# Two deformable layers: nine stored taps, the first batch on two queues, the fourth band convolved behind the first nine units

## The chip, the cores and the metric

One core of one Trainium2 chip runs the whole program in one launch. The metric is the device time of one execution in microseconds (us). All data are float32. The engines are TensorE (PE), VectorE (DVE), ScalarE (ACT), GpSimd (POOL) and SyncE (SP); each has its own list of instructions and they wait for each other by semaphores. DMAs are issued from the lists of SP, POOL and, in the changed kernel, ACT.

## The reference

The input is 8 images of 16 channels, 64 x 64. Four layers follow one another: a group norm with a gated scan, a mixture-of-experts inverted residual block, two deformable convolutions with group norm and a residual, and two "distance" convolutions. The change is in the two deformable layers alone, which are alike:

```python
off = conv2d(x, ow, ob).reshape(Bn, K, 2, Hh, Ww)      # K = 9 taps, an offset in y and one in x for each
cy = iy + dy + off[:, :, 0]; cx = ix + dx + off[:, :, 1]
samp = gather(y0i, x0i, (1-wy)*(1-wx)) + ...           # bilinear: four neighbours
out = einsum('bckhw,ock->bohw', samp, w) + b           # then norm over the image, relu, + x
```

## The kernel before, in words

A deformable layer (L is 0 or 1, called the first and the second pass here) does the gather as matrix products. The offsets come from a 3 x 3 convolution that is made in four bands m of 16 image rows. The rest is made in NB = 16 batches n of 4 rows, each in three units (parts of the image's width), 48 units a pass.

**The offsets' way.** PE convolves band m (`convolve`, L1487: 9 taps, 144 products, 288 records). ACT copies it from PSUM (`copy_offsets`, L1202, 4 instructions). DVE clips it (`bound_offsets`, L793 and L795) and, for the check for far taps, reduces the raw values (`reach`, L800). SP stores the clipped band in the DRAM tensor "offsets" (`store_offsets`, L503: 4 DMAs of 256 KB, with 16 planes an image and axis, of which 9 are taps). SP then copies from DRAM to DRAM what a batch needs into "offsets_by_batch" (`arrange_batch`, L520: 10 DMAs for batch 0, of which 4 serve image edges, and 6 for the others). POOL loads a batch to SBUF, each image's data repeated over the rows that need it (`load_batch`, L1737: 4 DMAs of 576 or 624 KB, both axes together, 2.3 to 2.5 MB a batch). There are three buffers for batches, so load n waits until DVE is done with batch n-3.

**The batches.** ACT turns a batch's x offsets into distances (`distances`, L1219) and writes |y| for a unit (`y_terms`, L1226). DVE finishes the distances (L812) and makes for each unit four products (L820 twice, L822, L823). PE multiplies them with windows of the image (`sample`, L1521, L1526); ACT copies the samples out of PSUM (`copy_samples`, L1239, L1242). After two batches PE contracts them with the layer's weights (`contract`, L1545, L1550); ACT and DVE write and add the resulting rows (`copy_rows` L1254, `add_shared_rows` L840). The products of a unit lie in a ring of three (RING), so y_terms of unit i+3 waits for PE's sample of unit i. The windows come from a copy of the image by columns: PE turns it (`turn_columns`, L1499), ACT and DVE copy it (`copy_columns`, L1192 and L1193, L784 and L785), POOL stores it (L1709) and loads windows (`load_windows`, L1724), ACT and DVE spread them (`spread_windows`, L1212 and L459).

**The order is written out by hand**, one list an engine, in the functions below. At a pass's start it is: PE convolve(0), turn_columns 0 to 7, convolve(1), (2), (3), then the units. ACT copy_offsets(0), copy_columns, copy_offsets(1), (2), distances(0), y_terms of units 0 to 2, spread_windows(0), copy_offsets(3), distances(1), spread_windows(1), then the units; before unit 6 it waits until all four bands are stored, because the samples of batches 2 and 3 take the place of the clipped offsets. DVE bound_offsets(0), copy_columns, reach(0), bound and reach of 1 and 2, spread_windows(0), batch 0, bound and reach of 3, then the batches. SP store(0), arrange 0, 1, 2, store(1), store(2), arrange 3, store(3), arrange 4 and so on. POOL store_columns, load_windows(0), load_batch(0), load_windows(1), load_batch(1), then a load for each batch and windows for every second.

## Time and profile before

| | |
|---|---|
| three runs | 735.8, 734.52, 729.37 us; median 734.52 us |
| the profiled execution | 729.7 us, of which the span of the profile is 727.5 us |
| mean granted clock of PE, as a share of full speed | 0.929 |
| busy share of the span: DVE, PE, ACT, POOL | 82%, 79%, 62%, 20% |
| first pass: last input row written, batch 0 begun on DVE (L812) | 174.0, 223.25 us |
| second pass: the same | 408.2, 461.63 us |

Times in rows are in us from the span's start, and durations are in us unless marked ns. A row of the timeline gives start, duration, engine, line, operation, tiles, the count of merged instructions, and in brackets how long the engine had been idle before it and what it waited for. In the chain of waits each row is a piece of the path that ended last. "SPq" and "POOLq" are DMA-issuing instructions.

### The profile page before, as it was taken

Reading aid. Unit: us, or ns where it says so; the run is one execution under the profiler, and the core shown is the slowest. Engines: PE = TensorE matmul, PEld = TensorE weight load, DVE = VectorE, ACT = ScalarE, POOL = GpSimd, SP = SyncE. Lnnn points to the kernel's source line nnn. Section 1 sums busy time; section 2 is a strip of 40 time slices with the busy share of each in tenths; the row PEclk is TensorE's granted clock in tenths of the full one; section 3 lists DMA queues with packets and bytes.
Section 4 is the critical chain, followed back from the end, with each engine's and each line's share of the span. In section 5 each row is a group of like instructions: output and inputs, shape, how many; then the busy total and the mean of one; then the engine's idle time right before and its main releaser. Section 6 shows DMA issues by size and latency. Waiting matters only on the chain.

```text
span 727.5 us, 29228 instructions
## 1 busy us (share of the span) xinstructions
PE 576.0 (79%) x13258; PEld 413.8 (57%) x13258; DVE 600.2 (82%) x853; ACT 453.1 (62%) x803; POOL 146.1 (20%) x258
## 2 busy tenths in 40 slices
PE   2719999999888698888886788669888888659491
PEld 1205887775654477666665454357666666537380
DVE  6998999942459999999998443999999999884866
ACT  2776774233227789999983412669999899251514
POOL 1005000010241343344200025134334420000000
PEclk9959999999988899999999798979999999969696
DMA  5004000000669898888730066979888862000003
GB/s 215 0 9 109 4 5 20 4 5 20 168 219 386 246 310 276 277 276 274 247 130 2 3 178 216 379 235 306 279 287 283 279 222 112 3 1 5 1 4 116
DMA packets 30198, 111.16 MB, mean 153 GB/s; under 512 B 11140, under 2 KB 15940, under 8 KB 25976
## 3 DMA queue, kind: packets, MB, share of 16 engines
q0 software_dynamic: 14912, 87.85, 35.8%
q1 hardware_dynamic: 15160, 21.42, 9.7%
q8 instruction: 105, 1.72, 1.0%
q14 instruction: 21, 0.17, 0.1%
HBM read 92.25 MB, written 19.65 MB: 154 GB/s over the span
## 4 chain that ended last, share of the span: by engine, by line
DVE 38%; PE 36%; DMA 10%; ACT 6%; issue 5%; SPq 2%; POOL 1%; DVEq 0%; ACTq 0%; POOLq 0%
PE psum L1433 12%; DVE arena L820 8%; DVE arena L822 7%; DVE arena L823 7%; DMA arena<-offsets_by_batch 7%; PE psum L1487 6%; PE psum L1642 6%; DVE arena L812 3%; PE psum L1521 3%; ACT arena L1212 2%; PE psum L1451 2%; PE psum L1652 2%; DMA offsets_by_batch<-offsets 1%; PE psum L1391 1%; SPq L520 1%
## 5 line engine op out<-in xcount | busy, mean ns | idle before, releaser
L1521 PE MATMUL psum<-arena 64*64 64x297 f32 (+4 forms) x4512 | 223.1, 340 | 48.3 <-DVE arena L823 40.9
L1521 PEld LDWEIGHTS psum<-arena 64*64 64x64 f32 x4512 | 171.1, 136 | 106.8 <-DVE arena L823 49.6
L1737 POOL DMA_DIRECT2D arena<-offsets_by_batch x128 | 78.1, 624 | 200.0 <-DVE arena L823 130.1
L1239 ACT ACTIVATE arena<-psum 128x396 f32<-128x396 f32 (+1 forms) x192 | 86.1, 509 | 36.4 <-PE psum L1521 24.0
L1487 PE MATMUL psum<-arena 32*32 32x512 f32 x2304 | 88.3, 651 | 22.7 <-issue 16.9
L820 DVE SCALAR_TENSOR_TENSOR arena<-arena 128x396 f32<-128x396 f32 (+1 forms) x192 | 98.2, 554 | 3.5 <-ACT arena L1226 2.5
L1433 PE MATMUL psum<-arena 32*32 32x512 f32 x2592 | 93.6, 597 | 0.0
L822 DVE SCALAR_TENSOR_TENSOR arena<-arena 128x792 f32<-128x792 f32 (+3 forms) x96 | 92.3, 961 | 0.0
L823 DVE SCALAR_TENSOR_TENSOR arena<-arena 128x792 f32<-128x792 f32 (+3 forms) x96 | 92.2, 960 | 0.0
L1545 PE MATMUL psum<-arena 64*64 64x256 f32 x1152 | 83.1, 381 | 2.6 <-ACT arena L1242 2.2
L1487 PEld LDWEIGHTS psum<-arena 32*32 32x32 f32 x2304 | 49.3, 107 | 59.3 <-issue 44.9
L1226 ACT ACTIVATE arena<-arena 128x792 f32<-128x792 f32 (+1 forms) x96 | 81.9, 857 | 0.0
L1219 ACT ACTIVATE arena<-arena 128x2304 f32<-128x2304 f32 (+1 forms) x32 | 71.6, 2236 | 12.3 <-DMA arena<-offsets_by_batch 12.3
L1433 PEld LDWEIGHTS psum<-arena 32*32 32x32 f32 x2592 | 65.1, 102 | 18.3 <-issue 3.5
L1212 ACT ACTIVATE arena<-arena 128x384 f32<-128x384 f32 (+2 forms) x124 | 65.1, 601 | 0.0
L1202 ACT ACTIVATE arena<-psum,arena 128x512 f32<-128x512 f32 x32 | 19.8, 687 | 67.9 <-PE psum L1487 67.8
L793 DVE TENSOR_SCALAR arena<-arena 128x2048 f32<-128x2048 f32 x8 | 10.8, 1347 | 56.6 <-ACT arena L1202 56.6
L716 DVE SCALAR_TENSOR_TENSOR arena<-arena 128x2048 f32<-128x2048 f32 x24 | 56.4, 2349 | 0.5
L1642 PE MATMUL psum<-arena 32*32 32x512 f32 x1152 | 44.4, 663 | 8.6 <-DVE arena L1022 8.6
L1545 PEld LDWEIGHTS psum<-arena 64*64 64x64 f32 x1152 | 43.9, 132 | 11.2 <-ACT arena L1242 2.4
L1151 ACT ACTIVATE arena<-psum,arena 128x512 f32<-128x512 f32 x48 | 34.2, 780 | 22.5 <-PE psum L1391 16.3
L812 DVE TENSOR_SCALAR arena<-arena 128x2304 f32<-128x2304 f32 (+1 forms) x32 | 43.7, 1366 | 1.7 <-ACT arena L1219 1.7
(169 smaller groups left out, 640.8 us busy)
## 6 DMA issues: line engine op xcount, KB each, us to landing
arena<-offsets_by_batch POOLq DMA_DIRECT2D x112, 576.0 KB, 7.9
arena<-offsets_by_batch POOLq DMA_DIRECT2D x16, 624.0 KB, 7.6
offsets<-arena SPq DMA_DIRECT2D x32, 256.0 KB, 10.0
offsets_by_batch<-offsets SPq DMA_DIRECT2D x184, 24.0 KB
arena<-columns POOLq DMA_DIRECT2D x24, 160.0 KB, 9.3
columns<-arena POOLq DMA_DIRECT2D x8, 320.0 KB, 6.7
arena<-in_x SPq DMA_DIRECT2D x4, 512.0 KB, 5.3
out<-arena SPq DMA_DIRECT2D x8, 256.0 KB, 2.2
```

The costliest lines, as they stand in the source:

```text
L820: v.scalar_tensor_tensor(own, own, 1.0, ap(tx + odd * W + u * TW, [[2 * W, KR // 2], [1, 2 * WB[u]]]), ALU.subtract, ALU.mult, reverse0=(o ...
L822: v.scalar_tensor_tensor(term(0), part(ty), 0.0, part(tx), ALU.max, ALU.mult)
L823: v.scalar_tensor_tensor(term(2), part(ty), 0.0, part(tx), ALU.min, ALU.mult).then_inc(s_g, 1)
L1212: ins = nc.scalar.activation(*spread_views(c, a, b, i), ACT.Copy, scale=con("image4", i, 1))
L1226: a.activation(ap(g_at(unit, 1), [[TW, KR], [1, 2 * WB[u]]]), ap(in_at(n, 1) + u * TW, [[W, KR], [1, 2 * WB[u]]]), ACT.Abs).then_inc(s_nd, 1)
L1239: ins = a.activation(ap(to + half * 2 * K * SX, [[SR, 2], [SX, 2 * K], [1, w]]), ap_ps(bank, [[CH, 2], [w, 2 * K], [1, w]], half * 2 * K * ...
L1433: ins = t_.matmul(ps_q(j, dw_bank(step) + i), cols(W_DIAG + (t * K + k) * Q, Q, Q * i, Q), ap(T_PAD[t % 4] + row * PW + k % 3, [[PW, CR], ...
L1487: ins = t_.matmul(ps_q(2 * axis + h, conv_bank(m) + i), cols(W_CONV[L] + (axis * K + t) * Q, Q, Q * i, Q), ap(XA + (BLK * m + 8 * h + t // ...
L1521: ins = t_.matmul(ps_t(s, bank + r, first * K * w, many * K * w), window, ap(g_at(unit, d0) + first * TW + s * w, [[GS + TW, many], [SLOTS ...
L1545: ins = t_.matmul(ps_t(r, bank, (2 - k // 3) * SX, GR * SX), weights_, ap(SAMP + j % 2 * SPAR + r * SR + k * SX, [[K * SX, GR], [1, SX]], ...
L1642: t_.matmul(ps_q(j, 4 * c + i), cols(W_DT[L] + k * P + Q * i, Q, Q * i, Q), at, start=(step == 0), stop=False)
L1737: g.dma_start(cols(in_at(n, 0), 2 * in_rows(n) * W, 64 * r + 32 * half, 32), bass.AP(batch_d.tensor, 2 * (4 * r * NB + n) * INS, [[0, QW / ...
```

## The change

It has five parts, the same in both passes.

1. The DRAM tensor "offsets" has 9 planes an image and axis in place of 16, and a row of zeros above and below each (written once, near the kernel's start, by 4 DMAs on SP). A band is stored by 8 DMAs of 9 partitions x 4 x 2 KB in place of 4 of 32 partitions. The DMAs for the edges at arranging go.
2. The first batch: SP stores, arranges and loads the x axis of band 0 and batch 0, ACT the y axis, each with its own DMAs (4 for the store, 4 to arrange, 4 to load). ACT does the store between copy_columns of groups 0 and 2, and arranging and loading before copy_offsets(1).
3. Every other batch is loaded by POOL with 8 DMAs, x first and then y, with a semaphore an axis; distances waits for x, y_terms of a batch's first unit for y. load_batch(1) now stands ahead of load_windows(1).
4. Band 2: ACT copies it after spread_windows(0), and DVE bounds and reduces it after batch 0 in place of before. Band 3: PE convolves one tap behind each of units 0 to 8, ACT copies it before unit 9, DVE reduces and bounds it after batch 4. The first contraction moves from units 6 to 10 to units 10 and 11, copy_rows(0) to unit 12.
5. SP's order becomes store(0), arrange 0, load x of batch 0, arrange 1, 2, store(1), arrange 3, 4, store(2), arrange 5 to 8, store(3), arrange 9 and on. ACT waits before unit 6 for bands 0 to 2 alone, and before unit 27 for band 3.

```diff
@@ -223,7 +223,7 @@
         xt_d = nc.dram_tensor("columns", [2, XQ, 4, H, C], F32, kind="Internal").ap()
-        off_d = nc.dram_tensor("offsets", [2, B * KP, H, W], F32, kind="Internal").ap()
+        off_d = nc.dram_tensor("offsets", [2, B * K, H + 2, W], F32, kind="Internal").ap()
         batch_d = nc.dram_tensor("offsets_by_batch", [B, NB, 2 * INS], F32, kind="Internal").ap()
@@ -315,7 +317,7 @@
         def conv_bank(m):
-            return 4 if m % 2 == 0 else 0
+            return 0 if m == 1 else 4
         HALF = N // 2
@@ -420,12 +422,14 @@
         def in_count(L, n):
-            return 64 * ((NB + 2 - n % 3) // 3 * L + n // 3 + 1)
+            if n == 0:
+                return 64 * (L + 1)
+            return 64 * ((NB - 1) // 3 * L + (n + 2) // 3)
         def arranged(L, n):
-            return 32 * ((14 if n % 4 in (0, 3) else 12) * L + 3 * (n // 4 + 1) + (2 if n % 4 == 0 or n == NB - 1 else 0))
+            return 32 * ((9, 12, 12, 13)[n % 4] * L + 3 * (n // 4 + (n % 4 > 0)) + (n == NB - 1))
         def g_at(unit, d):
@@ -471,7 +475,39 @@
                      ap_ps(bank, [[SX, rows], [1, WB[2]]], rho * SX + 2 * WB[0])))
+        def bounded_at(m):
+
+            return RAW + NATS if m == 3 else D1 + m % 2 * NATS
+
+        def store_part(eng, L, m, axis):
+
+            for h in range(2):
+                for b in range(2):
+                    eng.dma_start(bass.AP(off_d.tensor, (axis * B + b) * K * PLANE + W + (2 * m + h) * CH,
+                                          [[PLANE, K], [2 * K * PLANE, 4], [1, CH]]),
+                                  ap(bounded_at(m), [[CH, 4], [1, CH]], 64 * axis + Q * h + KP * b, K)
+                                  ).then_inc(s_ds[m], 16)
+
+        def arrange_first(eng, axis):
+
+            for ky, at, step, row, rows in ((-1, 0, SLOTS, 1, SLOTS), (0, 3 * SLOTS, SLOTS, 0, SLOTS),
+                                            (1, 6 * SLOTS, SLOTS, -1, SLOTS), (-1, KR, 1, 0, 1)):
+                eng.dma_start(bass.AP(batch_d.tensor, (axis * ER + at) * W, [[2 * NB * INS, B], [step * W, 3], [1, rows * W]]),
+                              bass.AP(off_d.tensor, (axis * B * K + 3 * (ky + 1)) * PLANE + (row + 1) * W,
+                                      [[K * PLANE, B], [PLANE, 3], [1, rows * W]])).then_inc(s_af[axis], 16)
+
+        def load_part(eng, n, axis):
+
+            for half in range(2):
+                for r in range(2):
+                    eng.dma_start(cols(in_at(n, axis), in_rows(n) * W, 64 * r + 32 * half, 32),
+                                  bass.AP(batch_d.tensor, 2 * (4 * r * NB + n) * INS + axis * in_rows(n) * W,
+                                          [[0, QW // 2], [2 * NB * INS, 4], [1, in_rows(n) * W]])
+                                  ).then_inc(s_in[n % 3][axis] if n else s_fl[axis], 16)
+
         UNITS = NB * NU
+        PLANE = (H + 2) * W
+        OWN_TAPS = NU * 3
         @block.sync
@@ -488,6 +524,10 @@
                                  cols(T_PAD[3], H * C, 0, 4 * HALO)).then_inc(s_zp, 16)
+            for axis in range(2):
+                for row in (0, H + 1):
+                    sp.dma_start(bass.AP(off_d.tensor, axis * B * K * PLANE + row * W, [[PLANE, B * K], [1, W]]),
+                                 cols(T_PAD[0], W, 0, B * K)).then_inc(s_oz, 16)
             for pair in (0, 2):
@@ -498,17 +538,13 @@
                 sp.wait_ge(s_d1, 4 * L + m + 1)
-                for axis in range(2):
-                    for h in range(2):
-                        sp.dma_start(bass.AP(off_d.tensor, axis * B * KP * N + (2 * m + h) * CH,
-                                             [[N, 2 * KP], [2 * KP * N, 4], [1, CH]]),
-                                     ap(D1 + m % 2 * NATS, [[CH, 4], [1, CH]], 64 * axis + Q * h, Q)
-                                     ).then_inc(s_ds[m], 16)
+                for axis in ((0, 1) if m else (0,)):
+                    store_part(sp, L, m, axis)
             def arrange_batch(L, n):
-                sp.wait_ge(s_ds[min(SLOTS * n + SLOTS, H - 1) // BLK], 64 * (L + 1))
+                sp.wait_ge(s_ds[min(SLOTS * n + SLOTS, H - 1) // BLK], 128 * (L + 1))
                 if n >= 4:
@@ -519,20 +555,11 @@
                                              [[2 * NB * INS, B], [step, 3], [1, rows * W]]),
-                                     bass.AP(off_d.tensor, (axis * B * KP + 3 * (ky + 1)) * N + row * W,
-                                             [[KP * N, B], [N, 3], [1, rows * W]])).then_inc(s_ar[n % 4], 16)
+                                     bass.AP(off_d.tensor, (axis * B * K + 3 * (ky + 1)) * PLANE + (row + 1) * W,
+                                             [[K * PLANE, B], [PLANE, 3], [1, rows * W]])).then_inc(s_ar[n % 4], 16)
                 for ky in (-1, 0, 1):
-                    row = SLOTS * n - ky
-                    first, end = max(row, 0), min(row + SLOTS, H)
-                    at = 3 * (ky + 1) * SLOTS * W
-                    taps(ky, at + (first - row) * W, SLOTS * W, first, end - first)
-                    if first > row:
-                        taps(ky, at, SLOTS * W, first, 1)
-                    if end < row + SLOTS:
-                        taps(ky, at + (end - row) * W, SLOTS * W, end - 1, 1)
-                if n == 0:
-                    taps(-1, KR * W, W, 0, 1)
+                    taps(ky, 3 * (ky + 1) * SLOTS * W, SLOTS * W, SLOTS * n - ky, SLOTS)
                 if n == NB - 1:
@@ -540,21 +567,27 @@
             sp.dma_start(cols(W_S64[0], K * 64), offset_weights[0, :, 2 * K * Q:]).then_inc(s_ws, 16)
+            sp.wait_ge(s_oz, 64)
             for L in range(2):
                 store_offsets(L, 0)
-                arrange_batch(L, 0)
+                sp.wait_ge(s_ds[0], 128 * (L + 1))
+                arrange_first(sp, 0)
+                sp.wait_ge(s_af[0], 64 * (L + 1))
+                load_part(sp, 0, 0)
                 arrange_batch(L, 1)
...
                 store_offsets(L, 1)
+                arrange_batch(L, 3)
+                arrange_batch(L, 4)
                 store_offsets(L, 2)
-                arrange_batch(L, 3)
+                for n in range(5, 9):
+                    arrange_batch(L, n)
                 store_offsets(L, 3)
-                arrange_batch(L, 4)
+                arrange_batch(L, 9)
                 sp.wait_ge(s_am, L + 1)
                 sp.dma_start(flag_d, cols(FMAX, 8)).then_inc(s_fd, 16)
-                for n in range(4, NB):
-                    if n + 1 < NB:
-                        arrange_batch(L, n + 1)
+                for n in range(10, NB):
+                    arrange_batch(L, n)
                 sp.wait_ge(s_fd, 16 * (L + 1))
@@ -691,6 +724,8 @@
                 first, end = (0, HALF_ROWS) if half == 0 else (HALF_ROWS, PW)
+                if t == 0:
+                    dve.wait_ge(s_oz, 64)
                 dve.wait_ge(s_relu, NCH * t + (5 if half == 0 else NCH))
@@ -787,9 +822,9 @@
                 dve.wait_ge(s_cve, 16 * L + 4 * m + 4)
-                if m >= 2:
-                    dve.wait_ge(s_ds[m - 2], 64 * (L + 1))
-                raw, d1 = RAW + m % 2 * NATS, D1 + m % 2 * NATS
+                if m == 2:
+                    dve.wait_ge(s_ds[0], 128 * (L + 1))
+                raw, d1 = RAW + m % 2 * NATS, bounded_at(m)
                 link(v.tensor_scalar(cols(d1, NATS), cols(raw, NATS), con("minus_limit"), con("limit"), ALU.max,
@@ -991,16 +1026,19 @@
                 reach(L, 0)
-                for m in (1, 2):
-                    bound_offsets(L, m)
-                    reach(L, m)
+                bound_offsets(L, 1)
+                reach(L, 1)
                 for n in range(NB):
...
                     if n == 0:
+                        bound_offsets(L, 2)
+                        reach(L, 2)
+                    if n == 4:
+                        dve.wait_ge(s_cve, 16 * (L + 1))
+                        reach(L, 3)
                         bound_offsets(L, 3)
-                        reach(L, 3)
                     j = n // 2 - 2
@@ -1214,13 +1252,15 @@
             def distances(L, n):
-                act.wait_ge(s_in[n % 3], in_count(L, n))
+                act.wait_ge(s_in[n % 3][0] if n else s_fl[0], in_count(L, n))
                 tx = cols(in_at(n, 0), in_rows(n) * W)
...
                 n, u = divmod(unit, NU)
+                if u == 0:
+                    act.wait_ge(s_in[n % 3][1] if n else s_fl[1], in_count(L, n))
                 if unit >= RING:
@@ -1259,23 +1299,36 @@
                 for g_ in (0, 2, 4, 6):
+                    if g_ == 2:
+                        if L == 0:
+                            act.wait_ge(s_oz, 64)
+                        act.wait_ge(s_d1, 4 * L + 1)
+                        store_part(a, L, 0, 1)
                     copy_columns(L, g_)
+                act.wait_ge(s_ds[0], 128 * (L + 1))
+                arrange_first(a, 1)
+                act.wait_ge(s_af[1], 64 * (L + 1))
+                load_part(a, 0, 1)
                 copy_offsets(L, 1)
-                copy_offsets(L, 2)
                 distances(L, 0)
...
                 spread_windows(L, 0)
-                copy_offsets(L, 3)
+                copy_offsets(L, 2)
                 distances(L, 1)
...
                     if unit == 2 * NU:
-                        for m in range(4):
-                            act.wait_ge(s_ds[m], 64 * (L + 1))
+                        for m in range(3):
+                            act.wait_ge(s_ds[m], 128 * (L + 1))
+                        act.wait_ge(s_red, 4 * L + 3)
+                    if unit == 9 * NU:
+                        act.wait_ge(s_ds[3], 128 * (L + 1))
                         act.wait_ge(s_red, 4 * (L + 1))
+                    if unit == OWN_TAPS:
+                        copy_offsets(L, 3)
                     copy_samples(L, unit)
@@ -1283,8 +1336,8 @@
                         spread_windows(L, n + 2)
-                    if u == NU - 1 and n % 2 == 1 and n >= 3:
-                        copy_rows(L, n // 2 - 1)
+                    if n >= 3 and (n % 2 == 1 and u == NU - 1 and n > 3 or unit == 4 * NU):
+                        copy_rows(L, n // 2 - 1 if n > 4 else 0)
                 copy_rows(L, NM - 1)
@@ -1477,10 +1530,10 @@
             for L in range(2):
-                def convolve(m):
+                def convolve(m, first=0, end=K):
                     pe.wait_ge(s_xa, NCH * L + max(min(2 * m + 3, NCH), 4))
-                    for t in range(K):
+                    for t in range(first, end):
                         for i in range(4):
@@ -1567,14 +1620,18 @@
                 pe.wait_ge(s_cve, 16 * L + 8)
-                convolve(3)
-                pe.wait_ge(s_cve, 16 * (L + 1))
                 pe.wait_ge(s_ws, 16)
...
                     step = NU * (n % 2) + u
-                    if n >= 2 and 2 * step < K:
+                    if unit < OWN_TAPS:
+                        pe.wait_ge(s_cve, 16 * L + 12)
+                        convolve(3, unit, unit + 1)
+                    if unit in (OWN_TAPS + 1, OWN_TAPS + 2):
+                        pe.wait_ge(s_cve, 16 * (L + 1))
+                        contract(0, 0 if unit == OWN_TAPS + 1 else 5, 5 if unit == OWN_TAPS + 1 else K)
+                    if n >= 4 and 2 * step < K:
                         contract(n // 2 - 1, 2 * step, min(2 * step + 2, K))
@@ -1732,12 +1789,8 @@
                     pool.wait_ge(s_g, UNITS * L + NU * (n - 2))
-                for half in range(2):
-                    for r in range(2):
-                        g.dma_start(cols(in_at(n, 0), 2 * in_rows(n) * W, 64 * r + 32 * half, 32),
-                                    bass.AP(batch_d.tensor, 2 * (4 * r * NB + n) * INS,
-                                            [[0, QW // 2], [2 * NB * INS, 4], [1, 2 * in_rows(n) * W]])
-                                    ).then_inc(s_in[n % 3], 16)
+                for axis in range(2):
+                    load_part(g, n, axis)
             for pair in (1, 3):
@@ -1751,9 +1804,8 @@
                 load_windows(L, 0)
-                load_batch(L, 0)
+                load_batch(L, 1)
                 load_windows(L, 1)
-                load_batch(L, 1)
                 for n in range(NB):
```

## Rows read from the trace of the kernel before

**Rows 1.** The page: busy time, share and instructions of each engine

```profile
PE 576.0 (79%) x13258; PEld 413.8 (57%) x13258; DVE 600.2 (82%) x853; ACT 453.1 (62%) x803; POOL 146.1 (20%) x258
```

**Rows 2.** The chain of waits in the first pass, from band 0 clipped to batch 0

```profile
187.52 0.34 SPq L503
...
189.12 8.03 DMA offsets<-arena
...
203.99 2.03 DMA offsets_by_batch<-offsets
...
208.23 12.59 DMA arena<-offsets_by_batch
```

**Rows 3.** DVE's timeline in the first pass

```profile
204.73 1.35 DVE L793 TENSOR_SCALAR arena<-arena 128x2048 f32<-128x2048 f32 x1 [12.36 <-ACT arena L1202]
...
214.63 1.35 DVE L793 TENSOR_SCALAR arena<-arena 128x2048 f32<-128x2048 f32 x1 [4.04 <-ACT arena L1202]
...
220.42 1.09 DVE L459 TENSOR_SCALAR arena<-arena 128x96 f32<-128x96 f32 x4
223.25 1.46 DVE L812 TENSOR_SCALAR arena<-arena 128x2496 f32<-128x2496 f32 x1 [1.74 <-ACT arena L1219]
...
240.03 1.35 DVE L812 TENSOR_SCALAR arena<-arena 128x2304 f32<-128x2304 f32 x1
...
249.45 1.35 DVE L812 TENSOR_SCALAR arena<-arena 128x2304 f32<-128x2304 f32 x1
...
338.16 0.48 DVE L840 TENSOR_TENSOR arena<-arena,psum 128x44 f32<-128x44 f32 x4 [0.56 <-ACT arena L1254]
...
377.09 1.46 DVE L812 TENSOR_SCALAR arena<-arena 128x2496 f32<-128x2496 f32 x1
```

**Rows 4.** DVE's timeline in the second pass

```profile
441.33 1.35 DVE L793 TENSOR_SCALAR arena<-arena 128x2048 f32<-128x2048 f32 x1 [14.32 <-ACT arena L1202]
...
461.63 1.44 DVE L812 TENSOR_SCALAR arena<-arena 128x2496 f32<-128x2496 f32 x1
...
478.39 1.35 DVE L812 TENSOR_SCALAR arena<-arena 128x2304 f32<-128x2304 f32 x1
...
614.32 1.46 DVE L812 TENSOR_SCALAR arena<-arena 128x2496 f32<-128x2496 f32 x1
```

**Rows 5.** SP's timeline, first pass, then the second

```profile
197.16 15.32 SPq L520 DMA_DIRECT2D offsets_by_batch<-offsets  x22
212.53 8.10 SPq L503 DMA_DIRECT2D offsets<-arena  x8
229.79 4.61 SPq L520 DMA_DIRECT2D offsets_by_batch<-offsets  x6
...
422.19 2.87 SPq L503 DMA_DIRECT2D offsets<-arena  x4
```

**Rows 6.** POOL's timeline, first pass

```profile
318.66 3.07 POOL L1737 DMA_DIRECT2D arena<-offsets_by_batch  x4 [7.02 <-DVE arena L823]
```

**Rows 7.** ACT's timeline, second pass

```profile
439.45 1.85 ACT L1202 ACTIVATE arena<-psum,arena 128x512 f32<-128x512 f32 x3 [4.93 <-PE psum L1487]
...
456.56 2.38 ACT L1219 ACTIVATE arena<-arena 128x2496 f32<-128x2496 f32 x1 [1.76 <-DMA arena<-offsets_by_batch]
```

**Rows 8.** PE's timeline, first pass

```profile
189.31 7.62 PE L1487 MATMUL psum<-arena 32*32 32x512 f32 x216
...
253.74 2.36 PE L1521 MATMUL psum<-arena 64*64 64x99 f32 x48 [1.33 <-DVE arena L823]
```

**Rows 9.** Page: costliest groups (busy us, mean ns | idle before)

```profile
L1545 PE MATMUL psum<-arena 64*64 64x256 f32 x1152 | 83.1, 381 | 2.6 <-ACT arena L1242 2.2
```

**Rows 10.** One stretch: us, PE, PEld, DVE, ACT, POOL busy, PEclk, DMA share, GB/s

```profile
213.00:230.00 17.00, 12.39 (x278) 5.47 (x264) 13.56 (x16) 9.75 (x15) 4.66 (x8) 0.90 1.03 386
```

**Rows 11.** Page: DMA issues (count, KB each, median us from issue to landing)

```profile
arena<-offsets_by_batch POOLq DMA_DIRECT2D x112, 576.0 KB, 7.9
...
offsets<-arena SPq DMA_DIRECT2D x32, 256.0 KB, 10.0
```

6 lines of the change are left out of this document (4 added, 2 removed).

## The prediction

> **What bounds the kernel now.** I read the page's first part, then the chain of waits, then each engine's timeline at the start of both passes. VectorE is the busiest engine, 82% of the span, with TensorE at 79% [rows 1]. Inside the batches of a deformable layer VectorE hardly stops: one batch takes 9.42 us (249.45 - 240.03), and from batch 1 to batch 15 there are 14 of these and five L840 groups of 0.39 us, 133.8 us; the rows say 137.06 us in the first pass and 135.93 us in the second [rows 3, 4]. So 3.2 and 2.1 us are stalls, small ones as in the L840 row, which waited 0.56 us for ScalarE [rows 3]. After the first few units a pass can only be shortened by starting batch 0 earlier, by taking VectorE work out of the loop, or by removing those 5.3 us.
>
> Batch 0 starts at 223.25 and 461.63 [rows 3, 4]. In the first pass the chain up to it is transfers: band 0 is clipped at 187.5, stored at 197.1, arranged at 206.0, loaded at 220.8 [rows 2]; ScalarE then needs 2.4 us for the distances. In the second pass the load too was awaited (ScalarE 1.76 us, until 456.56) [rows 7], and VectorE clipped and reduced band 2 right up to the start. VectorE's price for one band, clip and reduce, is 220.42 - 214.63 = 5.8 us [rows 3].
>
> **The change, part by part.**
>
> *Band 2 moves behind batch 0.* This is the part that costs. Its 5.8 us stood in a stretch where VectorE was idle 4.04 us just before and waited for the load just after; now they stand in a loop that is bound by VectorE. Band 3 stays inside the loop, later: nothing. Cost 5.8 us a pass, fixed, 11.6 us in all. Lower end 5.8 (same instructions), upper 6.8 (as the gap after batch 0 now, 240.03 - 223.25 - 9.9 = 6.9, with its extra small pieces).
>
> *Store of band 0.* Now four 256 KB DMAs, last piece landing 9.6 us after the first issue [rows 2]. Then 4 x 72 KB on each of SP and ACT, 576 KB in all for 1 MB. Issue is 2.87 us for four on a queue [rows 5], both queues at once. ScalarE's own column copies come after its four issues, so the column store by POOL begins some 3 us later and competes less. I take 7.0 us (issue, then 4.1); ends 5.9 and 9.6. Gain 2.6 us.
>
> *Arranging batch 0.* Ten issues and a landing, 197.1 to 206.0, 8.9 us; an issue costs 15.32/22 = 0.70 us [rows 5], the landing 2.03 us [rows 2]. With four issues on each queue: 4 x 0.65 + 2.0 = 4.6 us. Gain 4.3 us; ends 2.5 (if the column store slows it) and 4.5.
>
> *Loading batch 0.* Now 206.3 to 220.8, 14.5 us [rows 2]. The bytes stay 2.5 MB. Other loads no longer stand beside it, because batch 1 is arranged behind it in SP's queue; but the best row is 7.9 us a DMA after its issue [rows 11], and three loads together moved 386 GB/s with the DMA engines full [rows 10]. So 10 us is the lower end, 16 the upper. I take 14, near the only row of this very load. Gain 0.5 us.
>
> First pass: 223.25 - 2.6 - 4.3 - 0.5 = 215.9. The other condition is band 1: ScalarE copies groups 2 to 6 only after its store, so convolve(1), which began at 189.31 [rows 8], starts 1.7 us later (191.0), and VectorE's L793 moves from 204.73 [rows 3] to 206.4; with 5.8 us and 1.1 us of spread_windows batch 0 could start at 213.3, so the load decides. Second pass: clipped at 422.19 [rows 5] + 7.0 + 4.6 + 14 + 2.4 = 450.2, and by band 1 441.33 + 1.7 + 5.8 + 1.1 = 449.9 [rows 4]; 450.2 stands. Starts 7.4 and 11.4 us earlier, less 5.8 each: gains of 1.6 and 5.6 us, 7.2 in all. The second pass gains more because band 2's convolution, which ended at about 452 there, leaves the path.
>
> The Trainium skill, "DMA: Bandwidth & Descriptors", section "Issuing engines are not separate DMA queues", says that DMAs from several engines run on the same 16 DMA engines and that issuing from two saves only sequencer time. Rows 10 agree, since there the share was full whoever had issued. By it the two queues are worth only the issue time, which is how I count them.
>
> *Convolution of band 3, tap by tap.* 9.8 us of TensorE for nine taps (9.82 us for the 288 records that begin with L1487 of a band; the row of 216 records in 7.62 us gives 10.2) [rows 8], 1.1 us a tap. A unit's sampling is 2.36 us [rows 8], so 3.5 us beside VectorE's 3.14 us a unit (9.42/3). Over units 3 to 8 TensorE falls behind by about 2 us at most, and the first contraction, 83.1/16 = 5.2 us [rows 9] over two units instead of five, adds another 3 us at unit 11. The ring of three units gives some 3 us of slack, and VectorE's 6 us for band 3 after batch 4 lets TensorE catch up. I take 0.25 us a pass; ends -0.5 (nothing and a smoother start) and 3.
>
> *Load in two halves.* POOL issues 8 DMAs for 4, 0.6 us each, so y lands later by up to 2.4 us but x earlier, and ScalarE needs y only after distances, spread_windows and one copy, about 5 us on. Issue had taken 3.07 us after the wait for VectorE [rows 6]; the load that began there reached ScalarE 14.5 us later, just too late. So most of the 5.3 us of stalls should go: I take 3; ends 0 and 5.3. The earlier arranging of batch 4 works the same way.
>
> *ScalarE's wait before unit 6.* Here is a new wait. ScalarE must not write batch 2's samples until bands 0 to 2 are stored; everything behind it on ScalarE (copy_samples(6), y_terms(9)) is queued, and VectorE needs y_terms(9) for batch 3. Band 2 is now clipped after batch 0, and its store stands in SP's list behind arrange 3 and 4, which wait for band 1 to be stored. First pass: x load issued at 202.0, arrange 1 and 2 (12 x 0.70) until 210.4, store(1) (8 x 0.72) until 216.2, landed 17.3 us after its first issue as before (212.53 to 229.79) [rows 5] at 227.7, arrange 3 and 4 (12 x 0.77) until 236.9, store(2) until 242.6, landed 10.0 us on [rows 11] at 252.6. VectorE's batches: 215.9 + 9.9 + 5.8 + 0.7 = 232.3 for batch 1, 241.7, and 251.1 for batch 3, whose unit 9 begins at 252.5. y_terms(9) is ready at 252.6 + 1.8 = 254.4: 1.9 us late. I take 1.8 us in each pass, 3.6 together; ends 0 and 6 us a pass. Where the stores land with less traffic it is nothing.
>
> The zero rows are four DMAs of SP in the 50 us before the first layer's results: nothing.
>
> Sum: 7.2 + 3.0 - 3.6 - 0.5 = 6.1 us. On the profiled execution, 729.7 us (span 727.5 us), that is 723.6; that execution is 4.8 us under the median of 734.5 us, which the forecast is made against: 728.4 us. A measurement of this kernel can tell about 1%, 7.3 us, from no change.
>
> **The rivals.**
>
> *A: everything falls well.* The load of batch 0 lands in 10 us, the stores in time, no wait before unit 6, no stalls. Then band 1 decides both starts (213.3 and 449.9: 2.6 + 0.3 us more), 3.6 us of wait and 2.3 us more of stalls go: 6.1 + 8.8 = 14.9, so 719.6 us. For it: transfers had idle engines beside them before. Against it: the load alone took 14.5 us.
>
> *B: the transfers gain nothing but issues.* Store of band 0 still 9.6 us, load 15.3 us (2.5 MB at half of 386 GB/s is 12.9, + 2.4). Starts are 3.9 us later in each pass than I take: 6.1 - 7.8 = -1.7, so 736.2 us. For it: each new store has 9 partitions for 32, and the loads go to another kind of queue. The Trainium skill, same page, section "Why a DMA increments its semaphore by 16 and not by 1", says that the number of DMA engines of one DMA is the largest divisor up to 16 of both sides' outermost sizes, and on SP's and ACT's queues always the lowest ones: 9 engines for a store, 8 for the first load, the same 8 for x and y. No row of this trace shows single engines. By the rule B is what happens.
>
> *C, the slower side: the wait before unit 6.* If bands land as late as store(1) did (17.3 us from first issue, behind loads), or SP is held longer by arrange 3 and 4, band 2 lands 8 us later than I take, about 260, and the stall is 9.8 us a pass in place of 1.8: 6.1 - 16 = -9.9, so 744.4 us. It decides from 3 us a pass beyond my value, where the gain is gone. For it: SP's list has six items before store(2). Against it: the store has little more than half the bytes, and 8 us is long.
>
> **How the numbers follow.** Forecast 0.43, with 724 to 733 its own range; A 0.20, B 0.23, C 0.14. The likeliest is 728.4. The range goes from 716 (A with a little more) to 739 (B and the near part of C). Faster by over 1%: all of A and half of the forecast, 0.41. Slower by over 1%: C and a little else, 0.14. Within 1%: 0.45.
>
> **What would show it.** Right: batch 0's L812 near 216 in the first pass, and near 450 in the second; a band of L793, L795, L800 of 5.8 us after batch 0; two gaps of 6 us in the L812 spacing, after batches 0 and 4; ScalarE idle before unit 6 (a releaser "DMA offsets<-arena") of a few us; no ScalarE wait for loads after batch 5. Wrong: batch 0 not earlier (B), a gap of over 5 us before batch 3 (C), an L812 spacing of over 9.8 us in batches 1 to 4 from TensorE's taps, or VectorE's instructions longer beside POOL's doubled issues.

## The result: 1.5% slower, and the profile after

The kernel after took 742.05 us (median of four, 741.27 to 743.06) beside 732.87 us for the kernel before (also a median of four). The two medians divide to 1.0125; the ratio on record, taken over runs in the fast state alone, is 1.0149 (95%: 1.0111 to 1.0187). The forecast was 728.4 us, the range ended at 739. The profiled execution took 741.27 us, of which the span is 739.5 us, 12.0 us more than before.

The page, first part, answers to [rows 1]:

```profile
PE 571.9 (77%) x13258; PEld 407.0 (55%) x13258; DVE 599.9 (81%) x853; ACT 451.0 (61%) x803; POOL 216.5 (29%) x370
```

No engine does more work than before but POOL, which issues nearly twice as many loads (240 for 128). So the 12 us are waiting, and they are sorted by place. A pass is cut here at four points of VectorE: the last input row written (174.04 before, 174.83 after), batch 0's first instruction, batch 15's first instruction, and the end of the residual addition (before 408.22 and 645.10, after 414.47 and 656.44). In us:

| | first pass, before, after | second pass, before, after |
|---|---|---|
| input ready to batch 0 | 49.2, 47.1 | 53.4, 49.0 |
| batch 0 to batch 15 | 153.8, 161.7 | 152.7, 162.2 |
| batch 15 to the end | 31.1, 30.9 | 30.8, 30.8 |
| pass | 234.2, 239.6 (+5.5) | 236.9, 242.0 (+5.1) |

The start came 2.2 and 4.4 us earlier, where I had 7.4 and 11.4; the batches cost 7.8 and 9.5 us more, where I had 5.8 + 1.8 + 0.25 - 1.5 = 6.4. Both halves of the sum failed, the first one more: 12.2 of the 16.7 us between the forecast (6.1 us less) and the two passes (10.6 us more).

**The start.** SP's timeline, first pass, beside [rows 5]:

```profile
188.38 2.60 SPq L486 DMA_DIRECT2D offsets<-arena  x4
194.12 5.11 SPq L495 DMA_DIRECT2D offsets_by_batch<-offsets  x4
204.66 2.78 SPq L503 DMA_DIRECT2D arena<-offsets_by_batch  x4
```

POOL's timeline of the same stretch:

```profile
192.85 4.88 POOL L1766 DMA_DIRECT2D columns<-arena  x8 [34.48 <-ACT arena L1231]
201.39 2.54 POOL L1781 DMA_DIRECT2D arena<-columns  x4 [3.66 <-DMA columns<-arena]
```

ScalarE's timeline of it:

```profile
194.12 5.63 ACTq L495 DMA_DIRECT2D offsets_by_batch<-offsets  x4
204.90 3.00 ACTq L503 DMA_DIRECT2D arena<-offsets_by_batch  x4
207.95 2.42 ACT L1240 ACTIVATE arena<-psum,arena 128x512 f32<-128x512 f32 x4 [15.13 <-issue]
219.47 2.38 ACT L1257 ACTIVATE arena<-arena 128x2496 f32<-128x2496 f32 x1 [9.11 <-DMA arena<-offsets_by_batch]
```

The steps can be read off the starts. Store: 188.37 to 194.12, 5.75 us (forecast 7.0). Arranging: 194.12 to 204.66, 10.5 us (forecast 4.6), longer than the 8.9 us of ten DMAs on one queue. Load: 204.66 to 219.47, 14.8 us (forecast 14). So the arranging is where the time stays. Its four issues alone last 5.11 us (1.28 us each; an issue was 0.70 us in [rows 5]), and POOL's store of the columns, which began at 189.44 before, now begins at 192.85 and so lies on top of it: the DMA engines' share is 0.92 between 194.1 and 204.7 us. In the second pass the steps are 5.55, 10.4 and 15.9 us.

**The batches.** VectorE's timeline at batches 3 to 5 of the first pass, with the pauses:

```profile
257.07 1.35 DVE L847 TENSOR_SCALAR arena<-arena 128x2304 f32<-128x2304 f32 x1
260.28 1.05 DVE L855 SCALAR_TENSOR_TENSOR arena<-arena 128x396 f32<-128x396 f32 x2 [1.86 <-ACT arena L1266]
...
268.31 1.35 DVE L847 TENSOR_SCALAR arena<-arena 128x2304 f32<-128x2304 f32 x1
272.43 1.05 DVE L855 SCALAR_TENSOR_TENSOR arena<-arena 128x396 f32<-128x396 f32 x2 [2.77 <-ACT arena L1266]
...
280.46 2.27 DVE L835 TENSOR_REDUCE arena<-arena 128x32 f32<-128x2048 f32 x1
...
286.66 1.35 DVE L847 TENSOR_SCALAR arena<-arena 128x2304 f32<-128x2304 f32 x1
```

L847 is a batch's start (L812 before). The band's pause after batch 4 is 286.66 - 280.46 = 6.2 us in the first pass; the one after batch 0, which held band 3 before, now holds band 2 (16.37 us from batch 0 to 1, before 16.78). Two stalls are new: 1.86 us before unit 9 and 2.77 us before unit 12, each for y_terms (L1266). On ScalarE it stands behind distances and windows, which follow the copy of a batch's last samples (units 5 and 8), and that copy had waited for TensorE 1.44 and 1.07 us. TensorE's timeline shows why (L1574 are samples, L1540 the taps):

```profile
242.52 3.90 PE L1574 MATMUL psum<-arena 64*64 64x99 f32 x48 [3.50 <-DVE arena L858]
246.35 1.17 PE L1540 MATMUL psum<-arena 32*32 32x512 f32 x32
247.45 2.35 PE L1574 MATMUL psum<-arena 64*64 64x99 f32 x48
249.73 1.16 PE L1540 MATMUL psum<-arena 32*32 32x512 f32 x32
250.82 2.06 PE L1574 MATMUL psum<-arena 64*64 64x90 f32 x48
252.81 1.17 PE L1540 MATMUL psum<-arena 32*32 32x512 f32 x32
253.91 2.36 PE L1574 MATMUL psum<-arena 64*64 64x99 f32 x48
256.19 1.17 PE L1540 MATMUL psum<-arena 32*32 32x512 f32 x32
```

A unit with its tap takes 3.37 and 3.09 us (247.45, 250.82, 253.91), 3.28 on average, where VectorE takes 3.14, so TensorE cannot catch up. It was late by unit 3 alone: after 3.50 us of waiting for VectorE this sample took 3.90 us in place of 2.35, at a granted clock of 0.57 (242.5 to 246.4 us), near its lower level of 1.2 GHz. The six units 3 to 8 took it 21.2 us (242.52 to 263.75) for VectorE's 18.8. ScalarE's timeline shows what stands between two copies at a batch's end:

```profile
263.51 0.82 ACT L1266 ACTIVATE arena<-arena 128x720 f32<-128x720 f32 x1
264.21 2.21 ACT L1257 ACTIVATE arena<-arena 128x2304 f32<-128x2304 f32 x1
266.31 2.15 ACT L1250 ACTIVATE arena<-arena 128x384 f32<-128x384 f32 x4
268.36 2.41 ACT L1240 ACTIVATE arena<-psum,arena 128x512 f32<-128x512 f32 x4
270.63 0.96 ACT L1279 ACTIVATE arena<-psum 128x396 f32<-128x396 f32 x2
271.43 0.89 ACT L1266 ACTIVATE arena<-arena 128x792 f32<-128x792 f32 x1
```

From 264.21 to 270.63 ScalarE makes distances, windows and the copy of band 3, 6.4 us before the next copy of samples and its y_terms. From batch 5 on the loop is nearly free of stalls (0.8 and 1.0 us a pass, in batch 6). The wait before unit 6 shows nowhere: ScalarE's idle times there are for TensorE.

### The profile page after: what moved, and what is told of

It is laid out like the page before. It is cut to its first block, busy times and chain, and to the rows that moved or that the text cites. A ratio compares the mean times of both kernels' runs of the same rounds, so it can differ in the third digit from the quotient of the medians.

```text
span 739.5 us, 29433 instructions
## 1 busy us (share of the span) xinstructions
PE 571.9 (77%) x13258; PEld 407.0 (55%) x13258; DVE 599.9 (81%) x853; ACT 451.0 (61%) x803; POOL 216.5 (29%) x370
## 4 chain that ended last, share of the span: by engine, by line
DVE 41%; PE 38%; DMA 8%; ACT 7%; issue 4%; SPq 2%; ACTq 0%; DVEq 0%
PE psum L1486 11%; DVE arena L855 9%; DVE arena L857 8%; DVE arena L858 8%; PE psum L1574 7%; PE psum L1699 6%; PE psum L1540 4%; DVE arena L847 4%; DMA arena<-offsets_by_batch 4%; DMA offsets_by_batch<-offsets 2%; PE psum L1504 2%; PE psum L1709 2%; PE psum L1444 1%; PE psum L1428 1%; ACT arena L1250 1%
## 5 line engine op out<-in xcount | busy, mean ns | idle before, releaser
L1574 PE MATMUL psum<-arena 64*64 64x297 f32 (+4 forms) x4512 | 224.2, 342 | 70.1 <-DVE arena L858 68.4
L1574 PEld LDWEIGHTS psum<-arena 64*64 64x64 f32 x4512 | 170.6, 137 | 142.4 <-DVE arena L858 56.5
L503 POOL DMA_DIRECT2D arena<-offsets_by_batch x240 | 149.0, 649 | 148.3 <-DVE arena L858 99.1
L855 DVE SCALAR_TENSOR_TENSOR arena<-arena 128x396 f32<-128x396 f32 (+1 forms) x192 | 98.1, 552 | 10.4 <-ACT arena L1266 9.3
L1486 PE MATMUL psum<-arena 32*32 32x512 f32 x2592 | 93.7, 597 | 0.0
L1540 PE MATMUL psum<-arena 32*32 32x512 f32 x2304 | 83.2, 622 | 12.4 <-DVE arena L1060 5.8
L1598 PE MATMUL psum<-arena 64*64 64x256 f32 x1152 | 78.3, 381 | 6.8 <-ACT arena L1240 4.7
L1266 ACT ACTIVATE arena<-arena 128x792 f32<-128x792 f32 (+1 forms) x96 | 82.2, 860 | 2.0 <-DMA arena<-offsets_by_batch 2.0
L1486 PEld LDWEIGHTS psum<-arena 32*32 32x32 f32 x2592 | 65.6, 103 | 17.9 <-issue 3.7
L1540 PEld LDWEIGHTS psum<-arena 32*32 32x32 f32 x2304 | 40.5, 104 | 38.1 <-issue 21.9
L847 DVE TENSOR_SCALAR arena<-arena 128x2304 f32<-128x2304 f32 (+1 forms) x32 | 43.6, 1363 | 10.2 <-ACT arena L1257 10.2
L1699 PE MATMUL psum<-arena 32*32 32x512 f32 x1152 | 44.4, 663 | 8.6 <-DVE arena L1060 8.6
L1598 PEld LDWEIGHTS psum<-arena 64*64 64x64 f32 x1152 | 42.0, 132 | 15.1 <-ACT arena L1240 5.1
```

The source lines that it names most:

```text
L503: eng.dma_start(cols(in_at(n, axis), in_rows(n) * W, 64 * r + 32 * half, 32), bass.AP(batch_d.tensor, 2 * (4 * r * NB + n) * INS + axis * ...
L847: link(v.tensor_scalar(cols(tx, rows * W), cols(tx, rows * W), 1.0, 1.0, ALU.min, ALU.subtract))
L855: v.scalar_tensor_tensor(own, own, 1.0, ap(tx + odd * W + u * TW, [[2 * W, KR // 2], [1, 2 * WB[u]]]), ALU.subtract, ALU.mult, reverse0=(o ...
L1266: a.activation(ap(g_at(unit, 1), [[TW, KR], [1, 2 * WB[u]]]), ap(in_at(n, 1) + u * TW, [[W, KR], [1, 2 * WB[u]]]), ACT.Abs).then_inc(s_nd, 1)
L1486: ins = t_.matmul(ps_q(j, dw_bank(step) + i), cols(W_DIAG + (t * K + k) * Q, Q, Q * i, Q), ap(T_PAD[t % 4] + row * PW + k % 3, [[PW, CR], ...
L1540: ins = t_.matmul(ps_q(2 * axis + h, conv_bank(m) + i), cols(W_CONV[L] + (axis * K + t) * Q, Q, Q * i, Q), ap(XA + (BLK * m + 8 * h + t // ...
```

## The experiments

Ratios are to runs of the kernel before on the same chip. Kernels 1 to 6 and 8 to 11 start from the kernel after, 7 and 12 from the kernel before. The runs come from several launches, each with its own runs of the kernel before, whose medians lie between 728.88 and 733.52 us; where two changed kernels are compared, their profiled passes (cut as in the table above) are the better measure, since they leave out the rest of the program.

**1. All 16 DMA engines for the first load.** The theory was that the load, whose DMAs have outermost sizes of 32 (partitions) and 8 (source), uses 8 of the 16 engines. A stretch of the kernel after inside this load seemed to say so (columns as in [rows 10]):

```profile
213.00:219.00 6.00, 0.00 (x0) 0.00 (x0) 4.28 (x6) 0.00 (x0) 0.00 (x0) 0.68 0.52 208
```

The Trainium skill ("DMA: Bandwidth & Descriptors", section "Why a DMA increments its semaphore by 16 and not by 1") says that a DMA runs on the largest number of engines up to 16 that divides the slowest dimension of both sides; an estimate from it is 8 engines here, a share of 0.5. The trace's 0.52 agrees.

```diff
+            if n == 0:
+                for r in range(2):
+                    eng.dma_start(cols(in_at(n, axis), in_rows(n) * W, 64 * r, 64),
+                                  bass.AP(batch_d.tensor, 2 * (4 * r * NB + n) * INS + axis * in_rows(n) * W,
+                                          [[0, QW], [2 * NB * INS, 4], [1, in_rows(n) * W]])
+                                  ).then_inc(s_fl[axis], 16)
+                return
             for half in range(2):
```

> The changed kernel, with the first batch's load written as 2 DMAs of 64 partitions an axis in place of 4 of 32; bytes and queues are the same. Theory: the load (14.8 and 15.9 us from its first issue until ScalarE could go on) runs at 208 GB/s with a DMA share of 0.52 because its outermost sizes (32 and 8) put it on 8 of the 16 DMA engines; with 64 and 16 it gets all 16, the share goes near 1, the load lands in 8 to 10 us, and batch 0 then waits only for VectorE's band 1 (about 217.5 for 221.9 in the first pass), 4 us earlier in each pass: about 734 us. Rival: one queue or the source in DRAM limits the rate, the share stays at 0.5 and the time at 742.

740.44 us, ratio 1.0108 (1.0025 to 1.0191). Two windows of it:

```profile
206.00:213.00 7.00, 5.33 (x166) 3.28 (x135) 4.36 (x3) 2.42 (x4) 0.00 (x0) 1.00 1.01 221
213.00:217.00 4.00, 0.00 (x0) 0.00 (x0) 2.48 (x5) 0.00 (x0) 0.00 (x0) 0.91 0.99 202
```

The share doubled, the rate did not: 202 GB/s for 208. The load took 14.6 us (203.60 to 218.25) for 14.8. The number of engines alone is not what holds it. A busy share says that engines have packets in hand, not that they move more.

**2. Band 3 convolved whole, at its place of before.**

```diff
                 convolve(2)
                 pe.wait_ge(s_cve, 16 * L + 8)
+                convolve(3)
+                pe.wait_ge(s_cve, 16 * (L + 1))
...
-                    if unit < OWN_TAPS:
-                        pe.wait_ge(s_cve, 16 * L + 12)
-                        convolve(3, unit, unit + 1)
```

ScalarE's copy of it moves with it, behind spread_windows(0); the conv's bank of before comes back.

> The changed kernel, with band 3 convolved in one piece ahead of the units and copied by ScalarE with band 2, as before the change; band 3 is still bounded after batch 4. Theory: the two new stalls of VectorE ahead of units 9 and 12 (1.9 and 2.8 us a pass) come from the taps on TensorE and from the copy of band 3 in ScalarE's ring, and go: about 9 us less over two passes, less some 1 to 2 us a pass if the units start later: 735 to 738 us. Rival: they come from the load's traffic or from something else, and the stalls stay: 742 us or more.

734.89 us, ratio 1.0051 (1.0008 to 1.0094), 7.2 us under the kernel after. The stall before unit 12 is gone and 0.51 us is left of the one before unit 9: batches 3 and 4 take 9.89 and 15.62 us for 11.24 and 18.35 (the band's pause in the second of each). VectorE's only waits between 240 and 300 us are:

```profile
257.74 1.05 DVE L855 SCALAR_TENSOR_TENSOR arena<-arena 128x396 f32<-128x396 f32 x2 [0.51 <-ACT arena L1266]
...
295.52 1.05 DVE L855 SCALAR_TENSOR_TENSOR arena<-arena 128x396 f32<-128x396 f32 x2 [0.50 <-ACT arena L1266]
```

By the profiled passes (237.6 and 239.1 us for 239.6 and 242.0) the difference is 4.9 us, by the medians 7.2; of the 8.1 us between the two profiled spans 3.2 lie outside the passes, where the edit changes nothing. The tap by tap order costs 2.5 us a pass by the passes, and at most 3.6; I had 0.25.

**3. Three taps behind each of the first three units,** in case it is their spreading and not their sum.

```diff
-        OWN_TAPS = NU * 3
+        OWN_TAPS = NU
-                        convolve(3, unit, unit + 1)
+                        convolve(3, 3 * unit, 3 * unit + 3)
```

The first contraction goes back to units 6 to 10.

> The changed kernel, with three taps of band 3 behind each of the first three units in place of one behind each of nine, the copy before unit 3, and the first contraction at units 6 to 10 as before the change. Theory: TensorE has room in batch 0 and in VectorE's 6 us for band 2 behind it, so the stalls ahead of units 9 and 12 go at no price: about 733 us. Rival: TensorE is cold there and late for unit 3, and a new stall of 2 to 4 us a pass stands after batch 1 has begun: 738 us or more.

741.94 us, ratio 1.0141 (1.0059 to 1.0222): no gain. The stall only moved, to batch 2's first unit (that batch took 13.58 us in both passes). VectorE's row:

```profile
252.44 1.05 DVE L855 SCALAR_TENSOR_TENSOR arena<-arena 128x396 f32<-128x396 f32 x2 [4.20 <-ACT arena L1266]
```

and ScalarE's, which had waited for unit 2's sample behind 96 tap records:

```profile
242.68 0.85 ACT L1279 ACTIVATE arena<-psum 128x360 f32<-128x360 f32 x2 [5.51 <-PE psum L1574]
```

**4. Band 2 bounded before batch 0 again, the taps kept.** (ScalarE copies it before distances(0) again.)

```diff
-                bound_offsets(L, 1)
-                reach(L, 1)
+                for m in (1, 2):
+                    bound_offsets(L, m)
+                    reach(L, m)
...
-                    if n == 0:
-                        bound_offsets(L, 2)
-                        reach(L, 2)
```

> The changed kernel, with band 2 copied before distances(0) and bounded and reduced before batch 0, as before the change. Theory: in the changed kernel VectorE idles 4.6 and 5.6 us ahead of batch 0 for the load, so band 2's 5.8 us fit there and batch 0 starts only 1 to 2 us later, and the loop is 5.8 us a pass shorter: about 733 us. Rival: what follows batch 0 is not ready (ScalarE's y_terms(3) came at 235.8 in the first pass), and half of it comes back as stalls of batch 1: 738 us.

744.0 us, ratio 1.0143 (1.0054 to 1.0232). Batch 0 began at 222.74, 0.9 us later than in the kernel after, and batch 0 to 1 took 10.57 us for 16.37: so 4.9 us should have been won. They went again at once: batches 1 to 4 took 54.1 us for 48.4 (batch 4 19.77 for 18.35, behind a wait for y_terms of 4.18 us). The pause for band 2 had been giving TensorE time for its taps (in the kernel after it had done the first three and waited 3.50 us for VectorE before unit 3). With the taps in the loop, the band's 5.8 us cost nothing; without them (run 8) they cost 4.2 to 5.2 us a pass. The two edits had to be undone together.

**5. The first load from another source,** as many bytes to the same places. The kernel leaves out the first batch's real offsets: it reads rows of the input x in their place.

```diff
+            if n == 0:
+                for half in range(2):
+                    for r in range(2):
+                        eng.dma_start(cols(in_at(n, axis), in_rows(n) * W, 64 * r + 32 * half, 32),
+                                      bass.AP(x.tensor, 4 * r * C * N + axis * W,
+                                              [[4 * N, QW // 2], [N, 4], [1, in_rows(n) * W]])
+                                      ).then_inc(s_fl[axis], 16)
+                return
```

> The changed kernel, with the first batch's load taking its bytes from 64 different rows of the input x in place of the arranged offsets, of which each image's row is read 16 times an axis; sizes, queues and engines stay (the first batch's offsets are then not the convolution's, a part of the computation that is replaced). Theory: with 16 engines the load still ran at some 200 GB/s at a share near 1, so the limit is the source: few DRAM rows read by all engines at once. Then with other rows on 8 engines the rate stays at the 208 GB/s that 8 engines give or rises a little, and this run says only that: 14 to 15 us. Rival: the limit was always the 8 engines and the earlier run lost its time elsewhere: also 14 to 15 us. If the load lands in under 11 us, 8 engines are no limit at all and the source alone is.

One run, 741.08 us. The load took 14.7 us (204.50 to 219.22), at 214 GB/s:

```profile
213.00:217.00 4.00, 0.00 (x0) 0.00 (x0) 3.78 (x6) 0.00 (x0) 0.00 (x0) 0.73 1.03 214
```

The share is 1.03 where the kernel after had 0.52 with the same sizes, so more than the source changed: this run is to be set beside run 1, which also had a full share, and 214 for 202 GB/s says that where the bytes come from does not matter much. (The source's two outer steps, 4 * N over 8 and N over 4, run on into one another and can be read as one dimension of 32, which may be why the engines were full; no run here shows it.)

**6. The column store waits until batch 0 is arranged.**

```diff
+                for axis in range(2):
+                    pool.wait_ge(s_af[axis], 64 * (L + 1))
                 store_columns(L, 0)
```

> The changed kernel, with POOL's store of the columns waiting until both axes of batch 0 are arranged. Theory: arranging took 10.5 us for four small DMAs a queue because the 2 MB column store, which the ScalarE store has pushed 3 us back, now runs beside it; without it arranging takes 5 to 6 us, and batch 0's load starts 5 us earlier, though the windows may then be late. Rival: the arranging is slow by itself (small rows between two places in DRAM on 8 engines, two queues), and still takes 9 to 10 us.

One run, 755.33 us, as a whole worse, since the windows came late and batch 0 began at 227.47. But it shows the arranging by itself. SP's timeline:

```profile
192.38 2.77 SPq L495 DMA_DIRECT2D offsets_by_batch<-offsets  x4
196.90 2.89 SPq L503 DMA_DIRECT2D arena<-offsets_by_batch  x4
```

4.5 us (4.4 in the second pass), with issues of 0.69 us and the DMA engines' share at 0.15: my 4.6 us were right for an arranging that has the DMA engines alone. The load, though, now had the column store beside it and took 18.2 us. The store's traffic is paid somewhere.

**7. The kernel before with one part of the change: loads in two halves, x and then y, each with its semaphore.**

```diff
-                for half in range(2):
-                    for r in range(2):
-                        g.dma_start(cols(in_at(n, 0), 2 * in_rows(n) * W, 64 * r + 32 * half, 32),
...
+                for axis in range(2):
+                    for half in range(2):
+                        for r in range(2):
+                            g.dma_start(cols(in_at(n, axis), in_rows(n) * W, 64 * r + 32 * half, 32),
...
```

> The kernel before, with one part of the change alone: every load in two halves, x first, with a semaphore an axis. Theory: the stalls of the late batches in the kernel before (3.2 and 2.1 us a pass) are waits for loads, x's half lands in time, and VectorE's L812 spacing becomes 9.42 and 9.82 us throughout: 3 to 5 us less than before. Rival: POOL's doubled issues make loads 1 and 2 later at the pass's start and give it back: no difference.

719.93 us, ratio 0.9813 (0.9774 to 0.9852): faster than the kernel before and the kernel after, and with run 12 the best of this study. VectorE's loop runs at 9.42 and 9.81 us a batch, but for one batch of the second pass (9.97). Batch 0 began at 219.90, 3.35 us before the kernel before, because x landed at 214.11; the start is now set by band 2 and not by the load:

```profile
213.10 1.35 DVE L793 TENSOR_SCALAR arena<-arena 128x2048 f32<-128x2048 f32 x1 [3.22 <-ACT arena L1202]
...
219.90 1.44 DVE L812 TENSOR_SCALAR arena<-arena 128x2496 f32<-128x2496 f32 x1
```

**8. The kernel after with the bands' order of before:** runs 2 and 4 together. Nine planes, two queues and split loads stay; band 3's bounding stays after batch 4.

> The changed kernel with both moves of bands undone (band 2 bounded before batch 0, band 3 convolved whole before the units and copied at once; it is bounded after batch 4); two queues, nine planes and split loads stay. Theory: the loop is 5.8 us a pass shorter, the taps' stalls are gone, and batch 0 starts within 1 us of the kernel before: about 3 us a pass faster than the run with band 3 convolved whole, near 728 us, equal to or a little better than the kernel before. Rival: batch 0 starts 3 us later in each pass, because ScalarE's DMA issues hold band 1 back, and the result is 2 to 5 us slower than before.

723.27 us, ratio 0.9852 (0.9812 to 0.9892). Against run 2 it differs by band 2 alone: 11.6 us by the medians, 9.4 by the profiled passes (232.4 and 234.9 us for 237.6 and 239.1). My cost was 5.8 us twice; from batch 0 to batch 15 it measures 6.2 and 4.1 us (153.2 and 154.1 for 159.5 and 158.2), and the start moves by 1.0 us at most (48.1 and 49.9 us after the input, for 47.1 and 49.9). Both moves of bands together cost the kernel after 14.3 us by the profiled passes, 18.8 by the medians.

**9. SP loads x first and then y, ScalarE neither.**

```diff
                 load_part(sp, 0, 0)
+                sp.wait_ge(s_af[1], 64 * (L + 1))
+                load_part(sp, 0, 1)
...
-                act.wait_ge(s_af[1], 64 * (L + 1))
-                load_part(a, 0, 1)
```

> The changed kernel, with y of batch 0 loaded by SP behind x, in place of by ACT beside it; ACT still stores and arranges y. Theory: whatever the number of DMA engines, one batch's load moves at 200 to 214 GB/s, so x and y side by side both land after 14.8 us; one after the other, x (1.25 MB) lands in 7 to 8 us, batch 0 starts when band 1 is reduced and the windows spread, near 217.5 for 221.9 in the first pass and some 5 us earlier in the second: 733 us, 9 less. Rival: one queue moves only half of what two move, x lands no earlier, and the time stays at 742 us or grows.

740.39 us, ratio 1.0132 (1.0074 to 1.0191). Batch 0 began at 216.48, near the forecast's 215.9, since x landed 9.8 us after its first issue (214.07). Then VectorE waited for y:

```profile
216.48 1.46 DVE L849 TENSOR_SCALAR arena<-arena 128x2496 f32<-128x2496 f32 x1 [6.34 <-ACT arena L1259]
221.12 1.05 DVE L857 SCALAR_TENSOR_TENSOR arena<-arena 128x396 f32<-128x396 f32 x2 [3.18 <-ACT arena L1268]
```

y landed at 220.15, as late as with two queues: one queue moved the 2.5 MB in 15.8 us, two in 14.8.

**10. Run 8 with the first batch back on one queue each** (SP stores and arranges, POOL loads x and y); nine planes stay.

```diff
-                for axis in ((0, 1) if m else (0,)):
+                for axis in (0, 1):
...
+                for axis in range(2):
+                    pool.wait_ge(s_af[axis], 64 * (L + 1))
+                    load_part(g, 0, axis)
```

> The run with the bands' order of before, and with the first batch taken back too: SP stores and arranges both axes (8 and 8 DMAs), POOL loads x and then y; nine planes, zero rows and split loads stay. Theory: the column store again runs beside the store of band 0 and not beside the arranging, x lands alone, and batch 0 waits only for band 2's reduction, as in the run with split loads on the kernel before: 718 to 722 us, so nine planes and zero rows are worth nothing by themselves. Rival: eight issues in place of four before band 0 has landed, and stores on fewer DMA engines, make later bands late: 725 us or more.

722.0 us, ratio 0.9863 (0.9799 to 0.9926): the same as run 8, so the two queues are worth nothing that can be told; nor are the nine planes, beside run 7's 719.93. SP's timeline shows the column store, issued at 189.61, on the other step this time:

```profile
187.76 7.17 SPq L486 DMA_DIRECT2D offsets<-arena  x8
202.61 5.36 SPq L495 DMA_DIRECT2D offsets_by_batch<-offsets  x8
```

The store of band 0 took 14.9 us (187.76 to 202.61) and the arranging 5.0 (POOL's load began at 207.57), 19.8 us together for the 16.3 of the kernel after and 18.8 before. For four microseconds POOL's queue moved far more at the same share than SP's and ScalarE's in run 1:

```profile
213.00:217.00 4.00, 3.37 (x111) 1.87 (x101) 2.31 (x2) 2.68 (x4) 1.94 (x4) 1.00 1.01 359
```

359 GB/s (with the windows' load among it) for run 1's 202. x landed at 215.94 and y at 220.74. The load as a whole was not much shorter: 13.2 us from the first issue to y (207.57 to 220.74) for run 1's 14.6, since between 207 and 213 us the rate was only 194 GB/s.

**11. The halves by queue:** SP loads both axes for partitions 0 to 63, ScalarE for 64 to 127, in case two DMAs to the same partitions hold each other up.

```diff
+        def load_rows(eng, r):
+            for axis in range(2):
+                eng.dma_start(cols(in_at(0, axis), in_rows(0) * W, 64 * r, 64),
...
-                load_part(sp, 0, 0)
+                sp.wait_ge(s_af[1], 64 * (L + 1))
+                load_rows(sp, 0)
...
-                load_part(a, 0, 1)
+                act.wait_ge(s_af[0], 64 * (L + 1))
+                load_rows(a, 1)
```

> The changed kernel, with the first batch's load divided between the queues by partitions and not by axis: SP loads x and then y to partitions 0 to 63, ACT to partitions 64 to 127, each DMA with 64 partitions. Theory: the earlier run with 64 partitions a DMA kept all DMA engines busy (share near 1) at only 200 to 213 GB/s because both queues wrote the same half of the partitions at the same time, first 0 to 63, then 64 to 127, and half of the memory's DMA ports can take no more; with both halves at once x lands in 5 to 6 us after the first issue, y 3 us later, the rate in the stretch is 330 GB/s or more, and batch 0 starts at band 1's time, about 217.5 in the first pass: 734 us. Rival: the two hardware queues are limited to some 210 GB/s together, the load still takes 14 us and the time stays at 740 to 742 us.

737.65 us (ten runs), ratio 1.0118 (1.0083 to 1.0152). x landed after 11.3 us (203.08 to 214.42), y 2.8 us later, at 228 GB/s between 213 and 217 us. Something, but no doubling. The run shows more about the loop: batch 0 began 3.4 and 6.3 us earlier than in the kernel after (43.7 and 42.7 us after the input), but the passes are only 1.3 and 1.0 us shorter (238.3 and 241.0 us). Most of the earlier start is given back as waits in the first five batches (0.64, 1.90 and 3.63 us for y_terms in the first pass; 2.82, 1.89 and 3.72 in the second, of which the first is for y of batch 0).

**12. Run 7, but distances waits for both halves,** to part "x first" from "smaller DMAs".

```diff
                 act.wait_ge(s_in[n % 3][0], in_count(L, n))
+                act.wait_ge(s_in[n % 3][1], in_count(L, n))
```

> The kernel before with every load in two halves, x first, but with distances waiting for both halves as it did for the whole. Theory: the gain of split loads (about 13 us, 720 us) comes from ScalarE going on when x has landed; with the wait for both it is gone, or turns into a small loss for POOL's doubled issues: 731 to 738 us. Rival: smaller DMAs as such keep the DMA engines better filled, and most of the gain stays, 722 us or less.

719.98 us, ratio 0.9826 (0.9775 to 0.9876): by the medians all of run 7's gain without using x early. By the profiled passes (230.9 and 233.6 us) it is 6.6 us of run 7's 9.4, and the rest is the first start, where batch 0 began 48.4 us after the input (run 7 45.5, before 49.2). The kernel before had four waits for loads between 260 and 380 us (ScalarE's timeline):

```profile
264.49 2.22 ACT L1219 ACTIVATE arena<-arena 128x2304 f32<-128x2304 f32 x1 [0.64 <-DMA arena<-offsets_by_batch]
...
313.33 2.22 ACT L1219 ACTIVATE arena<-arena 128x2304 f32<-128x2304 f32 x1 [0.68 <-DMA arena<-offsets_by_batch]
...
333.20 2.22 ACT L1219 ACTIVATE arena<-arena 128x2304 f32<-128x2304 f32 x1 [1.01 <-DMA arena<-offsets_by_batch]
...
352.50 2.22 ACT L1219 ACTIVATE arena<-arena 128x2304 f32<-128x2304 f32 x1 [0.43 <-DMA arena<-offsets_by_batch]
```

Run 12 has none there. Its page lists the DMAs, beside 7.9 and 9.3 us in the kernel before:

```profile
arena<-offsets_by_batch POOLq DMA_DIRECT2D x224, 288.0 KB, 5.3
...
arena<-columns POOLq DMA_DIRECT2D x24, 160.0 KB, 6.1
```

DMAs of half the size land in two thirds of the time, and the windows' DMAs between them gain as much. The whole traffic is the same (254 for 258 GB/s over 260 to 380 us).

## Why the prediction was wrong, point by point

**The step that failed first: "Arranging batch 0 ... 4 x 0.65 + 2.0 = 4.6 us. Gain 4.3 us; ends 2.5 (if the column store slows it) and 4.5."** It took 10.5 us, a loss of 1.6 us where even my bad end was a gain. I had seen that ScalarE's four store issues push its column copies 3 us back, and booked that as a help for the store. The store did take less (5.75 us for 7.0), but the column store then fell on the arranging. Run 6 shows the 4.5 us without it, and run 10 the column store back on the store of the band: 14.9 us for that, 5.0 for the arranging. The step is 5.9 and 5.8 us at the two starts, 11.7 of the 16.7 us that the two passes missed (band 1 moves with it, since its copy stands behind ScalarE's load issues). To have it right would not have won as much: run 11 began 9.7 us earlier over both passes and its passes are 2.3 us shorter, so the loop's waits take most of an earlier start back, and the two errors do not simply add.

**The starts.** 7.4 and 11.4 us earlier were forecast, 2.2 and 4.4 came. First pass, 5.2 us missing: arranging 5.9, load 0.8, store -1.25. Second, 7.0 us missing: arranging 5.8, load 1.9, store -1.45. In the second pass 0.8 us more comes from the band's store, issued 14.7 us after the input (14.0 before); in the first 0.2 us too much is counted.

**"I take 0.25 us a pass" for the taps.** Measured 2.5 by the passes, at most 3.6 (run 2). The ring argument compared TensorE's 3.5 us a unit with VectorE's 3.14 and gave the ring 3 us of slack. TensorE's lateness was sized about right (2.4 us after unit 8, forecast 2), though by another way: the taps cost it less than I had, and unit 3 at the lower clock 1.5 us more. What failed is the slack: it left out that ScalarE's list, through which every slot is given back, holds 4.1 us of distances and windows (264.21 to 268.36) at each batch's end, and at unit 9 the band's copy too. The upper end I gave, 3, holds by the passes.

**Band 2's 5.8 us a pass** was about right where the taps are gone: 9.4 us in both passes between runs 2 and 8, 11.6 by the medians. It was the change's large fixed cost, and the 2.2 and 4.4 us that the starts gained could not pay it. That it would cost nothing beside the taps (run 4), so that the two moves have one price together, was not in the sum.

**The wait before unit 6, 1.8 us a pass,** was nothing: the stores landed in time, and rival C's mechanism did not occur. The result lies on C's side of the range, but not by C.

**The load, 14 us.** 14.8 and 15.9. Rival B's half share could be seen, but its reason fell in run 1: with a full share the rate stayed; its slow store (9.6 us) took 5.75. B's time of 736.2 us was missed too. What the forecast cited of the Trainium skill ("Issuing engines are not separate DMA queues", same page) was borne out by runs 9 (2.5 MB in 15.8 us from one queue, 14.8 from two) and 10.

**"So most of the 5.3 us of stalls should go: I take 3."** The stalls did go: alone, on the kernel before, the split takes 4.5 us out of the two loops (150.9 and 151.1 us for 153.8 and 152.7, run 7). What I had not counted are the starts, 3.8 and 1.2 us; in all it is worth 9.4 us of the profiled passes and 13.6 us of median. The reason was off: the smaller DMAs empty the loop (run 12), and x before y adds only to the first start. In the kernel after the split was there too and hid how much the rest cost: the other parts together lose some 20 us (481.6 us of passes against 461.7; 22 by the medians).

**What stays open.** Why the first load ran at 202 to 228 GB/s from SP's and ScalarE's queues, and for a while at 359 from POOL's. Neither the number of engines (run 1), nor the source (run 5), nor the partitions that two DMAs share (run 11) explains it alone. The same load from POOL's queue in the kernel after was not tried. That smaller DMAs land sooner at the same traffic was shown, why was not.

## What to carry to other kernels

When work is moved off a start into a loop that one engine bounds, it costs nearly its full length there (4.2 and 5.2 of 5.8 us); where a second edit makes the loop wait anyway, it may cost nothing, so edits are to be undone in pairs as well as singly. And the earlier start must be re-derived with every transfer at its new time, since issues put into a compute engine's list push back the transfers that wait for that engine, here onto the very step they were to shorten. A big transfer that is moved off one step must be looked for on the next. A ring's slack is what is left after everything that stands in the returning engine's list between two slots, not the difference of two engines' speeds. Try the small part of a change by itself: cutting large loads into smaller DMAs was worth 1.8%, and the rest of this change gave back more than that.

## What the runs showed of the hardware

- The busy share of the DMA engines and their rate are different things: share 0.52 at 208 GB/s (the kernel after), 0.99 at 202 (run 1), 1.03 at 214 (run 5, another source), 1.01 at 359 (run 10, with windows beside it), all for the first batch's load.
- An issue of the arranging took 0.69 us on SP and 0.79 on ScalarE with the engines nearly free (run 6, share 0.15), and 1.28 and 1.41 us beside POOL's column store (the kernel after, share 0.92).
- After 3.50 us without work TensorE's granted clock was 0.57 for the next 3.9 us, and a sample of 2.35 us took 3.90 (the kernel after, 242.5 to 246.4 us); after 14.0 us without work it was 0.50 between 222 and 230 us.
- DMAs of 288 KB landed after 5.3 us where those of 576 KB needed 7.9, at 254 and 258 GB/s in all (run 12 and the kernel before).
